# A decoder layer on one core: attention over V taken in four parts with two buffers, and score blocks at their own width

## The reference

```
x = x + gated_linear_attention(layernorm(x))       # 16 heads, key width 16, causal over 128 tokens
q = ln(x @ Wq + bq);  k, v = ...                   # cross attention, 16 heads of 32
p = softmax(q k' * scale)                          # 112 keys and 16 "dca" keys, each normed for itself
ctx = p @ v ;  x = x + ctx @ Wo + bo
x = x + top2_of_4_experts(layernorm(x))
```

## Time and profile before

| what | value |
|---|---|
| median of three runs | 1052.63 us |
| profiled execution, its time | 1052.63 us |
| its span, first to last instruction | 1050.9 us |
| PE busy | 932.2 us (89%) |
| DVE busy | 697.7 us (66%) |
| POOL busy | 499.1 us (47%) |
| ACT busy | 453.1 us (43%) |
| granted TensorE clock, mean | 0.937 |

### The profile page before, as it was taken

How to read it: one execution, slowest core, us unless ns; L and a number is a source line. 1 busy time by engine, 2 the same in 40 slices (tenths; PEclk the granted TensorE clock), 3 DMA queues, 4 the chain that set the end, 5 groups by cost and what they waited for, 6 DMA issues and landing times.

```text
span 1050.9 us, 19085 instructions
## 1 busy us (share of the span) xinstructions
PE 932.2 (89%) x7297; PEld 559.8 (53%) x7297; DVE 697.7 (66%) x1293; ACT 453.1 (43%) x754; POOL 499.1 (47%) x563
## 2 busy tenths in 40 slices
PE   3688999999999999999999663069999999999995
PEld 1446666766666766776676442034444444444342
DVE  6767677878887788778886545856554445345672
ACT  3444555565566655665555423122232333233210
POOL 1447677767677777767775720111070001003643
PEclk9788999999999999999999965569999999999998
DMA  8413000000000000000000006032335234335593
GB/s 289 133 51 128 4 15 18 5 17 17 15 2 17 17 14 14 6 17 14 17 2 14 11 12 229 26 115 83 118 90 191 80 121 160 100 100 198 159 243 121
DMA packets 40300, 78.39 MB, mean 75 GB/s; under 512 B 11378, under 2 KB 11650, under 8 KB 40258
## 3 DMA queue, kind: packets, MB, share of 16 engines
q1 hardware_dynamic: 35266, 63.13, 18.0%
q0 software_dynamic: 4992, 14.70, 5.1%
HBM read 64.16 MB, written 13.65 MB: 74 GB/s over the span
## 4 chain that ended last, share of the span: by engine, by line
PE 74%; DVE 7%; POOL 5%; issue 4%; DMA 4%; SPq 3%; ACT 1%; POOLq 0%; DVEq 0%; ACTq 0%
PE ps L1009 18%; PE ps L1010 17%; PE ps L1011 17%; PE ps L1015 6%; PE ps L1102 4%; PE ps L1181 3%; PE ps L1197 3%; POOL y_fetched L728 2%; PE ps L1206 2%; POOL hrs L596 2%; PE ps L1226 2%; DVE big L1674 1%; DMA y_fetched<-y_scratch,idx_get 1%; SPq L473 1%; PE ps L1114 1%
## 5 line engine op out<-in xcount | busy, mean ns | idle before, releaser
L596 POOL TENSOR_TENSOR hrs<-hve,neg_half 128x16 f32<-128x16 f32 x48 | 140.2, 2921 | 3.8
L982 ACT ACTIVATE big<-ps 128x512 f32<-128x512 f32 x64 | 38.2, 597 | 233.2 <-PE ps L1011 233.0
L1771 DVE TENSOR_SCALAR big<-big 128x512 f16<-128x512 f32 x64 | 27.8, 435 | 110.4 <-ACT big L982 110.3
L1009 PE MATMUL ps<-w2h,big 128*128 128x512 f16 x256 | 97.0, 379 | 2.5 <-DVE big L1363 2.5
L1009 PE MATMUL ps<-big,w1h 128*128 128x512 f16 x256 | 97.8, 382 | 1.4 <-DVE big L1363 1.4
L1011 PE MATMUL ps<-big,w1l 128*128 128x512 f16 x256 | 97.8, 382 | 0.0
L1010 PE MATMUL ps<-big,w1h 128*128 128x512 f16 x256 | 97.8, 382 | 0.0
L1010 PE MATMUL ps<-w2l,big 128*128 128x512 f16 x256 | 97.0, 379 | 0.0
L1011 PE MATMUL ps<-w2h,big 128*128 128x512 f16 x256 | 97.0, 379 | 0.0
L711 POOL DMA_INDIRECT big<-x_scratch,token_of x16 | 18.3, 1147 | 149.3 <-PE ps L1015 77.5
L728 POOL DMA_INDIRECT y_fetched<-y_scratch,idx_get x32 | 37.5, 1173 | 104.8 <-DMA y_scratch<-big 89.4
(11 more groups left out here) (305 smaller groups left out, 2530.5 us busy)
## 6 DMA issues: line engine op xcount, KB each, us to landing
wst<-in_w SPq DMA_DIRECT2D x28, 1024.0 KB, 5.2
x_scratch<-xn SPq DMA_DIRECT2D x16, 256.0 KB, 2.1
y_fetched<-in_w SPq DMA_DIRECT2D x4, 1024.0 KB, 13.4
out<-x_all SPq DMA_DIRECT2D x4, 1024.0 KB, 7.9
pr<-in_w_attn SPq DMA_DIRECT2D x3, 1024.0 KB, 8.4
x_all<-in_w_attn SPq DMA_DIRECT2D x3, 1024.0 KB, 11.7
x_all<-in_x SPq DMA_DIRECT2D x1, 3072.0 KB, 11.7
y_scratch<-big SPq DMA_DIRECT2D x3, 1024.0 KB, 6.1
```

The source lines that it names most:

```text
L596: pool.tensor_tensor(hrs[n][:, :], hve[n][:, :], neg_half[:, :], ALU.pow).then_inc(hdev[n], 1)
L982: act.activation(hg[f % 2], psum[f % 2][:, 512:1024], ACT.Gelu, scale=UN).then_inc(hg_r, 1)
L1009: nc.tensor.matmul(o, lh, rh, start=first, stop=False)
```

## The change

It has two parts.

**Score blocks.** a2_scores takes each block at its own width, 128, 96, 64 and 32 columns, where it was 128, 96, 96 and 96.

**Product with V.** It is split in four calls of four heads, b2_pv(s, 0) to b2_pv(s, 3), which stand between the other steps of the tick. b2_turn and b2_pv take the heads by a new function pv_heads(g): part g has the row positions rr = 2(g//2) and 2(g//2)+1 and the columns c = 2(g%2) and 2(g%2)+1. All parts are turned into d0 and copied to two buffers pT in turn; d1 is only written by the product. Parts 0 and 1 wait for the first half of the probabilities alone, parts 2 and 3 for the second. Turn r waits for the copy of part r-1, and the product r for the copy of part r. The semaphore pv_ps counts four for each batch, and those who wait for it wait for the fourth.

```diff
-        pT = [sb(f"pT{i}", [P, KC, L]) for i in range(KC)]
+        pT = [sb(f"pT{i}", [P, KC, L]) for i in range(2)]
...
-                after(sp, pv_ps, b, ago=2)
+                after(sp, pv_ps, b, nth=4, per=4, ago=2)
...
-                take(pT[r][:, :, :], cols(d1 if r % 2 else d0), 1.0, pT_r)
+                take(pT[r % 2][:, :, :], cols(d0), 1.0, pT_r)
...
-                after(act, pv_ps, s[0])
+                after(act, pv_ps, s[0], nth=4, per=4)
...
-                            w = max(KTW[i], 3 * BLK)
-                            o = psum[1][0:w, col:col + 256].rearrange("p (e t) -> p e t", e=2)[:, :, i * BLK:(i + 1) * BLK]
-                            last = nc.tensor.matmul(o, kt[par][rw, c, KTO[i]:KTO[i] + w],
+                            o = psum[1][0:KTW[i], col:col + 256].rearrange("p (e t) -> p e t", e=2)[:, :, i * BLK:(i + 1) * BLK]
+                            last = nc.tensor.matmul(o, kt[par][rw, c, KTO[i]:KTO[i] + KTW[i]],
                                                     qeo[par][rw, c * NBLK + i, :, :], start=True, stop=True)
...
+            def pv_heads(g):
+
+                return [(2 * (g // 2) + i, 2 * (g % 2) + c) for c in range(2) for i in range(2)]
+
             def b2_turn(s, r):
                 b, par, half = s
-                for rnd in range(2):
-                    after(pe, pr_r[rnd], b)
-                if r >= 2:
-                    after(pe, pT_r, b, nth=r - 1, per=4)
-                elif r == 1:
-                    after(pe, lg_r, b, ago=1)
+                after(pe, pr_r[r // 2], b)
+                if r:
+                    after(pe, pT_r, b, nth=r, per=4)
                 else:
                     after(pe, x2_r, b, ago=1)
-                ps = d1 if r % 2 else d0
                 pg = pr[par][:, :].rearrange("p (m n) -> p m n", n=L)
-                for rr in range(4):
-                    last = nc.tensor.transpose(ps[:, rr * L:(rr + 1) * L], pg[:, rr * KC + r, :], ident[:, :])
+                for i, (rr, c) in enumerate(pv_heads(r)):
+                    last = nc.tensor.transpose(d0[:, i * L:(i + 1) * L], pg[:, rr * KC + c, :], ident[:, :])
                 last.then_inc(pT_ps, 1)
 
-            def b2_pv(s):
-                b, par, half = s
-                after(pe, pT_r, b, nth=4, per=4)
+            def b2_pv(s, r):
+                b, par, half = s
+                after(pe, pT_r, b, nth=r + 1, per=4)
                 after(pe, vb_r, b)
-                for h in range(HEADS):
-                    c, rr = h // 4, h % 4
+                if r == 0:
+                    after(pe, lg_r, b, ago=1)
+                for i, (rr, c) in enumerate(pv_heads(r)):
+                    h = 4 * c + rr
                     last = nc.tensor.matmul(d1[32 * rr:32 * rr + 32, c * L:(c + 1) * L], vx[par][:, h * DV:(h + 1) * DV],
-                                            pT[c][:, rr, :], start=True, stop=True)
+                                            pT[r % 2][:, i, :], start=True, stop=True)
                 last.then_inc(pv_ps, 1)
...
                 on(s[3], b2_turn, 1)
+                on(s[3], b2_pv, 0)
                 on(s[0], a1_turn)
                 on(s[2], b1_kT)
                 on(s[3], b2_turn, 2)
+                on(s[3], b2_pv, 1)
                 on(s[1], a2_o)
                 on(s[3], b2_turn, 3)
                 on(s[0], a1_kg1)
+                on(s[3], b2_pv, 2)
                 on(s[2], b1_qT)
-                on(s[3], b2_pv)
+                on(s[3], b2_pv, 3)
                 on(s[1], a2_o_turn)
```

## The result

The changed kernel takes 1095.56 us (median, 1094.20 to 1101.68) where before takes 1053.36 in the same comparison: ratio 1.0413, 95% interval 1.0362 to 1.0465, so 42 us slower. Forecast was +28, 1081 us, with a range up to 1091: the direction was right, and so were the two costs that the forecast named, but a third one, the clock, was not in its sum. The profiled execution took 1098.96 us (span 1097.2), 46 us over that of before.

What follows compares the result with a forecast made beforehand. PE was taken to bound ticks 3 to 15 at clock 1.00: 13 x (0.86 + 1.14) = 26.0, with the ends 27.9 us, on 1052.6 gives 1080.5, said as 1081 us. Range 1067 to 1091.

Steps and rivals of the forecast that it cites:

- Changes of shape: On PE, starting matmuls of another array shape costs about 0.13 us inside a score call, five changes per call.
- a call: One a2_scores call, 32 matmuls: 2.04 us forecast for 1.61, +0.43, twice a tick.
- part 1: Score blocks at their own width: +0.86 us a tick, shape changes outweighing narrower weight loads.
- 64 columns are a shape apart from 128: Score blocks: 64 columns need a shape change; the rival without one gave 1063 us, 8 in 100.
- Matmuls in flight: Product with V: each quarter alternates two column groups, four rounds of two for two of four, +0.87 us a tick.
- The waits: Semaphore waits around turns and copies: relaxed and new ones cost nothing; rival of late copies, 1093 us, 9 in 100.
- Last tick: Tick 18: with one bank each turn waits for the copy before it, so the product ends 2.0 us later.
- both ends of the pipeline together: Ticks outside 3 to 15: +2.0 in tick 18, -0.9 in tick 17, +0.8 in tick 2, sum +1.9 us.
- Part 2: Product with V in four quarters: +0.87 us for rounds and +0.27 for shape changes, +1.14 us a tick.
- quarters 1 and 2: Product quarters beside a2_o and the 16-column product: they share existing shape changes, each four rounds of two, 0.436 us.
- The tick without a fall: Ticks 3 to 15, from 34.16 us to 36.1 us: +0.86 for score blocks and +1.14 for the product.
- PE's own time is the tick: Ticks 3 to 15: PE is busy throughout at clock 1.00, so added PE time is paid in full.

Runs made afterwards that it cites:

- e4: The changed kernel with score blocks of one width together (128, 128, 96, 96, 64, 64, 32, 32): ratio 1.0215 to before.
- e1: The kernel before with only the score blocks at their own width, the product with V in one call: ratio 1.0206 to before.
- e12: The kernel before with score blocks 128, 96, 64, 64, equal widths together, half the q projection inside the first score call: ratio 0.9986.
- e7: The kernel before with score blocks of 128, 96, 64, 64 columns, one width together: ratio 0.9987.
- e3: The changed kernel with each quarter of the product with V taking four heads of one column, so four column groups: ratio 1.0295 to before.
- e2: The changed kernel with score blocks back at 96 columns or more, the product with V still in four quarters: ratio 1.0169 to before.
- e8: The kernel before with six more dense 512-column float16 matmuls added in a1_g: ratio 1.0212.
- e6: The changed kernel with the first score call cut in two and half of the q projection between: ratio 1.0368 to before.
- e11: The kernel before with the first score call cut in two and half of the q projection between: ratio 1.0031.

## Why the prediction was wrong

**What held.** PE bounds ticks 3 to 15: it is busy 445.71 of 446 us there also after (114 to 560 us). Changes of shape: forecast 0.13 us each, e4 measures 0.13; a call forecast at 2.04 takes 2.06, so part 1 is +0.90 a tick, +0.91 in e1, for +0.86. 64 columns are a shape apart from 128, which no row of before showed: five changes fit the call, and the undivided call of e12 takes 1.54 us where e7's expectation gives 1.38 if they shared one. This is the drain of the Trainium skill's page TensorEngine Tiling (Array Packing), Key Properties; the trace agrees, at 0.13 us a change. Matmuls in flight: a quarter was forecast at 0.56 and is; e3 shows the cause. The waits: relaxed and new ones cost nothing in those ticks, as forecast. Last tick: +1.9 for +2.0; but both ends of the pipeline together, forecast at +1.9, grew by 5.6 us (2.2 and 3.4 in the ledger), with low clock in both, which is not taken apart further.

**What was mis-sized.** Part 2 was +1.14 and is +0.95 alone (e2) and about +0.93 beside part 1: quarters 1 and 2 do not stand beside a2_o and a1_kg1 but run into them. At 426.97 a matmul of a2_o starts ahead of quarter 1's last two, and at 429.19 quarter 2 begins among the 16-column matmuls. Quarter 2 with the 16-column product takes 1.01 us (428.74 to 429.75) where that product alone took 0.77 (331.08 to 331.85 in the earlier trace rows), so it adds 0.24 where 0.44 was forecast. Quarter 1 with a2_o takes 1.43 (426.72 to 428.15) for 1.02, so it adds 0.41. Work of one shape on other column groups overlaps across steps, which the forecast used inside a step and not between two. The tick without a fall so is +1.83 for +2.00.

**The step that failed** is the first one of all: "PE's own time is the tick", priced at the granted clock of 1.00 of the earlier trace rows. The sum multiplies instruction counts by durations at 2.4 GHz; no term and no rival had the clock fall. After, the q projection takes 4.60 us or more for 2.92 in 9 of 13 ticks, which makes up most of the 17.6 us in the ledger; the medians miss the forecast by 15 us and the profiled executions by 18. The forecast read 1.00 as a property of the phase, but it is a rounded mean over 444 us, in which 3.4 us at half clock don't show. The trace of before held a warning. The clock of 3.4 us in tick 4 of before, in the form of the earlier trace rows, and PE's timeline around it:

```profile
149.90:153.30 3.40, 3.40 (x14) 1.20 (x11) 2.24 (x4) 1.89 (x3) 3.06 (x5) 0.50 0.00 0
```

```profile
147.44 1.03 PE L1226 MATMUL ps<-wgate_sb,x3T 128*128 128x4 f32 x8
148.40 1.76 PE L1102 MATMUL ps<-qeo,kt 32*128 32x64 f32 x32
150.09 0.60 PE L1158 MATMUL ps<-bq,row_w 64*128 64x512 f16 x1
...
151.03 0.63 PE L1010 MATMUL ps<-wl,x2h 128*128 128x512 f16 x1
151.46 0.63 PE L1011 MATMUL ps<-wh,x2l 128*128 128x512 f16 x1
...
154.52 0.60 PE L1197 MATMUL ps<-ident,pr 128*128 128x128 f32 x4
```

With nothing changed the clock is 0.50 there, the q projection takes 4.43 us (150.09 to 154.52) for 2.92, and its matmuls follow each other by 0.43: a fall. Ahead of it lie the logits and the scores, 1.0 and 1.7 us of small matmuls. The change lengthens that stretch by 0.45 us and all ticks by 1.8; e2 and e8 show that a longer tick is enough for falls, with the stretch as it was or shorter.

**What stays open.** The same stretch with the same distances is followed by a fall in one tick and not in the next (e8). The cut removes the falls in three pairs, so the stretch in one piece is a cause; but which ticks are hit, why e6 still has them, and why after has more than either part alone, these runs do not settle. A single fall costs 1.69 us and a long one 3.2, but no rule here gives their number. One lead, not tested: in after every tick from 10 to 15 has a fall, and by the clock's record the low stretch begins 1.1 us behind the start of the q projection in tick 10 and 0.3 us in tick 15, drifting slowly against the tick, while before has none in ticks 5 to 15. How the loop lies in time seems to matter, and not only what is in it.

## What to carry to other kernels

On an engine that bounds, price three things apart from the matmul count: changes of array shape (0.13 us each here, so keep a width together and pad narrow blocks to the shape of their neighbours), how many neighbours in order use different parts of the array (two or four in flight is a factor of two), and the clock. A granted clock of 1.00 in the trace of before is not a margin: look in short windows, since the mean over the loop hid a fall here, for a single tick in which the dense work behind a stretch of small matmuls ran at half pace. Such a loop can lose more by a change of its length than the instruction counts say. Dense work in the middle of the stretch kept the clock up in five kernels here, but it cost 0.1 to 0.3 us a tick itself, paid clearly in one pair of three, and made the kernel before 3 us slower (e11).

## What the runs showed of the hardware

With 1 us of dense matmuls more in a tick, right ahead of the sparse stretch, the clock fell in 4 of 13 ticks, where it fell in one before (e8). Float32 products on two column groups ran among float16 products on another one without the 0.13 us of a change of shape; both have 128 rows and at most 32 columns (429.19 in the timeline above). And the clock fell without any idle time of PE: in e8 it is busy 14.00 of 14.00 us from 205 to 219, ahead of a fall. The Trainium skill (TensorE: Matmul & The Clock Gate, Why this matters for your kernels) warns of idle gaps between bursts; here there was no such gap, and the clock fell all the same.
